# Four graph layers and a Taylor step: more tile sums on VectorE, products in pairs, row sums from a column of ones

## The reference, cut to what matters

```python
# x: (2048, 64) f32, adj: (2048, 2048) int32
# layer 1 (layer 2 the same; layer 3 holds two attentions and a small MLP): x = x + gat(relu(layernorm(x)))
Wh = inputs @ W
e = (Wh @ a_src)[:, None] + (Wh @ a_dst)[None, :]
e = jnp.where(e > 0, e, ALPHA * e)
attention = jax.nn.softmax(jnp.where(adj > 0, e, NEG_BIG), axis=1)
return jax.nn.elu(attention @ Wh)

# last layer
h = h - h.mean(axis=-1, keepdims=True)
h = h / jnp.maximum(jnp.linalg.norm(h, axis=-1, keepdims=True), EPS)
k, q = h @ w_k, h @ w_q
a = adj * softmax(k @ q.T / sqrt(8))
a = a / a.sum(axis=-1, keepdims=True)
return (a + a @ a / 2 + (a @ a) @ (a @ a) / 6) @ h
```

## Time and profile before

| | |
|---|---|
| median of the runs | 630.39 us |
| the profiled execution's own time | 626.87 us |
| its span | 625.0 us |
| TensorE busy | 550.7 us (88%) |
| VectorE busy | 401.1 us (64%) |
| ScalarE busy | 285.6 us (46%) |
| L703, products | 138.6 us |
| L695, masks | 72.9 us |
| L722, sum passes of the loops | 51.1 us |
| L929, sum passes of the last stage | 8.5 + 8.5 us |
| share of TensorE in the chain that ended last | 68% |
| share of VectorE in it | 19% |

### The profile page before, as it was taken

How to read it: one execution, slowest core, us unless ns; L and a number is a source line. 1 busy time by engine, 2 the same in 40 slices (tenths; PEclk the granted TensorE clock), 3 DMA queues, 4 the chain that set the end, 5 groups by cost and what they waited for, 6 DMA issues and landing times.

```text
span 625.0 us, 7189 instructions
## 1 busy us (share of the span) xinstructions
PE 550.7 (88%) x2951; PEld 179.8 (29%) x2986; DVE 401.1 (64%) x530; ACT 285.6 (46%) x298; POOL 32.7 (5%) x29
## 2 busy tenths in 40 slices
PE   5545999988999988999788898999769999999997
PEld 3401112233112234212133112235332232333332
DVE  2986979546988645989747988543999995100000
ACT  1475555433746433656433756344858785100000
POOL 0500000202000101000000000021100000000000
PEclk9556899999999999999999999999997999999999
DMA  8891000000000000000000000000000000000000
GB/s 356 347 404 69 1 0 2 0 1 2 0 1 0 1 1 2 2 0 1 0 1 1 1 1 1 1 1 0 2 0 1 0 1 1 1 0 1 0 1 34
DMA packets 3183, 19.30 MB, mean 31 GB/s; under 512 B 336, under 2 KB 464, under 8 KB 1104
## 3 DMA queue, kind: packets, MB, share of 16 engines
q1 hardware_dynamic: 3008, 18.04, 7.1%
q10 hardware_dynamic: 144, 0.82, 0.4%
HBM read 18.33 MB, written 0.52 MB: 30 GB/s over the span
## 4 chain that ended last, share of the span: by engine, by line
PE 68%; DVE 19%; ACT 5%; issue 4%; DMA 2%; POOL 1%; POOLq 0%; DVEq 0%; SPq 0%; ACTq 0%
PE PROD L703 15%; PE PROD L914 9%; PE X L695 9%; PE X L914 9%; PE S L722 7%; DVE X L1194 4%; DVE aB L1436 3%; ACT big L409 3%; PE S L929 2%; DVE nadj L1315 2%; DVE big L1206 2%; DMA aB<-in_adjT 1%; PE M L581 1%; PE M L678 1%; DMA cst<-in_cst 1%
## 5 line engine op out<-in xcount | busy, mean ns | idle before, releaser
L409 ACT ACTIVATE big<-X,v 128x1024 f32<-128x1024 f32 x128 | 142.6, 1114 | 132.7 <-PE X L695 132.2
L1194 DVE SCALAR_TENSOR_TENSOR X<-wB,v,aB 128x1024 f32<-128x1024 f32 x128 | 163.9, 1294 | 23.6 <-ACT big L409 21.3
L703 PE MATMUL PROD<-big,Wh 128*64 128x512 f32 x512 | 138.6, 621 | 0.4 <-ACT big L409 0.2
L695 PE MATMUL X<-nadj,bigI 128*128 128x512 bf16 x234 | 72.9, 386 | 23.5 <-DVE X L1194 21.3
L722 PE MATMUL S<-big,onesf 128*32 128x512 f32 x384 | 51.1, 604 | 3.2 <-DVE big L1206 2.4
L695 PEld LDWEIGHTS X<-nadj,bigI 128*128 128x128 bf16 x256 | 14.6, 97 | 124.1 <-DVE X L1194 87.0
L703 PEld LDWEIGHTS PROD<-big,Wh 128*64 128x64 f32 x512 | 26.1, 135 | 66.2 <-issue 58.4
L914 PE MATMUL PROD<-big,Wh 128*64 128x512 f32 x128 | 32.8, 634 | 3.3 <-ACT big L509 3.2
L342 POOL TENSOR_TENSOR rr<-var,mhalf 128x8 f32<-128x8 f32 x8 | 17.5, 2187 | 328.2 <-DVE var L1058 328.2
L914 PE MATMUL PROD<-nadj,Wh 128*64 128x512 f32 x128 | 29.8, 599 | 0.0
L1206 DVE TENSOR_TENSOR big<-big 128x1024 f32<-128x1024 f32 x24 | 29.3, 1220 | 0.4
(11 more groups left out here) (276 smaller groups left out, 586.2 us busy)
## 6 DMA issues: line engine op xcount, KB each, us to landing
big<-in_adjT SPq DMA_DIRECT2D x13, 1024.0 KB, 7.9
aB<-in_adjT SPq DMA_DIRECT2D x3, 1024.0 KB, 8.2
cst<-in_cst ACTq DMA_DIRECT2D x1, 800.0 KB, 5.4
x<-in_xT SPq DMA_DIRECT2D x1, 512.0 KB, 6.1
out<-x SPq DMA_DIRECT2D x2, 256.0 KB, 2.0
late<-in_late SPq DMA_DIRECT2D x1, 208.5 KB, 9.8
```

Of the source, the lines that this page charges most:

```text
L409: act.activation(prob[:, t % U, :], X[t % 2][:], ACT.Exp, bias=v2[l % 2][:, k:k + 1]).then_inc(p_ready, 1)
L695: last = pe.matmul(X[t % 2][:, hh * BANK:(hh + 1) * BANK], bigI[:], nadj[:, k, half_cols(c, hh)], start=False, stop=True, skip_group_check ...
L703: last = pe.matmul(PROD[c][feat(hh), :], Wh[l % 2][:, k, :], prob[:, t % U, hh * BANK:(hh + 1) * BANK], start=k == 0, stop=k == NB - 1)
L1194: dve.scalar_tensor_tensor(X[t % 2][:], wB[:, cols(c)], v8[l % 2][:, k:k + 1], aB[:, cols(c)], ALU.max, ALU.add).then_inc(x_written, 1)
```

## The change

It does three things, and a few small ones that they need.

1. **Sums.** In chunk 1 the tiles 0 to 6 are added by VectorE instead of 0 to 4: two more adds of 128x1024, behind the exponents of tiles 7 and 8. The sum pass at tile 5 goes, five passes are left there instead of six.
2. **Pairs.** In the attention loop TensorE issues product k, product k+1, mask k+2, mask k+3. Only for p = 2 the order of before stays.
3. **Row sums of the last stage.** The sum passes L929 go. The last feature of h is replaced by 1, so that the product itself carries the row sums in the last row of each half. The last feature is the negative sum of the others, since a row of h has mean zero; a matrix `restore` puts it back: `turn` multiplies with it instead of transposing for n = 0 and 1, and one more matmul of 512 columns per chunk writes the restored z to S, which VectorE adds to x (`restored`) in place of the first `scaled` addition.

```diff
-        ADDED = ((0, 1, 4, 5, 10), (0, 1, 2, 3, 4))
-        ADD_BEHIND = ({3: (1,), 6: (4,), 8: (5,), 12: (10,)}, {3: (1,), 5: (2, 3), 7: (4,)})
-        ADDS = 4
-        FIRST_SUM = (3, 5)
+        ADDED = ((0, 1, 4, 5, 10), (0, 1, 2, 3, 4, 5, 6))
+        ADD_BEHIND = ({3: (1,), 6: (4,), 8: (5,), 12: (10,)}, {3: (1,), 5: (2, 3), 7: (4, 5), 8: (6,)})
+        FIRST_SUM = (3, 7)
...
-                act.wait_ge(a_summed, c + 1)
+                act.wait_ge(q_psum, c + 1)
...
-                act.activation(sT, S[:], ACT.Copy).then_inc(rowsum_ready, 1)
+                act.activation(sT, PROD[c][:], ACT.Copy).then_inc(rowsum_ready, 1)
...
-                        for i in range(2):
-                            products(l, c, k + i)
+                        if p == 2:
+                            for i in range(2):
+                                products(l, c, k + i)
+                                mask(l, c, k + 2 + i)
+                        else:
+                            products(l, c, k)
+                            products(l, c, k + 1)
                             if p < NB // 2 - 1:
-                                mask(l, c, k + 2 + i)
+                                mask(l, c, k + 2)
+                                mask(l, c, k + 3)
...
-                for strip in range(4):
-                    tile, hh = k - 1 + strip // 2, strip % 2
-                    last = pe.matmul(S[32 * strip:32 * strip + 32, :], onesf[:, 0:32],
-                                     kept(c, tile)[:, hh * BANK:(hh + 1) * BANK], start=k == 1, stop=k == NB - 1)
...
-                    last = pe.matmul((M, X[0])[c][:, 2 * bb:2 * bb + 2], sT[:, bb * P:(bb + 1) * P], pick,
-                                     start=True, stop=True)
+                    last = pe.matmul((M, X[0])[c][:, 2 * bb:2 * bb + 2], sT[:, bb * P:(bb + 1) * P],
+                                     ident[:, F - 1::F], start=True, stop=True)
...
-                    last = pe.transpose(back[n % 2][:, bb * P:(bb + 1) * P], z[n % 2][:, bb * P:(bb + 1) * P], ident)
+                    rows = z[n % 2][:, bb * P:(bb + 1) * P]
+                    if n < NCH:
+                        last = pe.matmul(back[n % 2][:, bb * P:(bb + 1) * P], rows, restore, start=True, stop=True)
+                    else:
+                        last = pe.transpose(back[n % 2][:, bb * P:(bb + 1) * P], rows, ident)
                 last.then_inc(zT_psum, 1)
+                if n < NCH:
+                    if n:
+                        pe.wait_ge(x_restored, n)
+                    pe.matmul(S[:], restore, z[n], start=True, stop=True).then_inc(restored_psum, 1)
...
+                dve.memset(Y[1][:, b, F - 1:F], 1.0).then_inc(y0_ready, 1)
...
+            def restored(c):
+
+                dve.wait_ge(restored_psum, c + 1)
+                signal(dve.tensor_tensor(x[:, c, :], x[:, c, :], S[:], ALU.add), x_restored, c + 1)
...
+            restored(0)
             row_reciprocals(1)
             for n in range(1, 4 * NCH):
                 scaled(n)
+                if n == 1:
+                    restored(1)
```

More of the change, by code:

```diff
@@ L41 @@
 WIDTH = _at
-LATE = {"mw": (0, 3 * P), "wkq": (3 * P, 4 * EMB), "mb": (3 * P + 4 * EMB, 1)}
-LATE_WIDTH = 3 * P + 4 * EMB + 1
+LATE = {"mw": (0, 3 * P), "wkq": (3 * P, 4 * EMB), "mb": (3 * P + 4 * EMB, 1),
+        "restore": (3 * P + 4 * EMB + 1, P)}
+LATE_WIDTH = 4 * P + 4 * EMB + 1
 def program(nc, xT_d, cst_d, late_d, adjT_d, out_d):
@@ L88, in program @@
         wkq, mb, win = const("wkq"), const("mb"), const("win")
+        restore = const("restore")
         wTt = const("wTt")[0:F].rearrange("p (l k) -> p l k", l=GAT)
@@ L250, in program @@
         a_ready = sem("a_ready")
-        a_summed = sem("a_summed")
+        restored_psum = sem("restored_psum")
+        x_restored = sem("x_restored")
         rowsum_ready = sem("rowsum_ready")
@@ L276, in added_by, with additions @@
         def added_by(c_all, k):
-            return ADDS * c_all + max(ADDED[c_all % NCH].index(k), 1)
+            return additions(c_all) + max(ADDED[c_all % NCH].index(k), 1)
+        def additions(c_all):
+            return sum(len(ADDED[m % NCH]) - 1 for m in range(c_all))
         def kept(c, k):
@@ L717, in sums @@
                 if k - 1 in ADDED[c]:
-                    pe.wait_ge(p_added, ADDS * (NCH * l + c + 1))
+                    pe.wait_ge(p_added, additions(NCH * l + c + 1))
                 for strip in range(4):
@@ L815, in _ @@
                             sums(l, c, k + 1)
-                        for i in range(2):
-                            products(l, c, k + i)
+                        if p == 2:
[5 more added lines that the diff above has]
+                            products(l, c, k + 1)
                             if p < NB // 2 - 1:
-                                mask(l, c, k + 2 + i)
+                                mask(l, c, k + 2)
+                                mask(l, c, k + 3)
                             elif c == 0:
-                                mask(l, 1, i)
+                                mask(l, 1, 0)
+                                mask(l, 1, 1)
                         if c == 0 or p < NB // 2 - 1:
@@ L922, in absorb @@
                     last.then_inc(q_psum, 1)
[L923 to L926, removed]
-                for strip in range(4):
-                    tile, hh = k - 1 + strip // 2, strip % 2
-                    last = pe.matmul(S[32 * strip:32 * strip + 32, :], onesf[:, 0:32],
-                                     kept(c, tile)[:, hh * BANK:(hh + 1) * BANK], start=k == 1, stop=k == NB - 1)
-                if k == NB - 1:
-                    last.then_inc(a_summed, 1)
             def row_totals(c):
@@ L972, in _ @@
             key_rows(1)
-            pe.wait_ge(y0_ready, 1)
+            pe.wait_ge(y0_ready, 2)
             first_turn(1)
@@ L983, in _ @@
                 if k == LAG - 1:
-                    pe.wait_ge(y0_ready, 2)
+                    pe.wait_ge(y0_ready, 4)
                     max_columns(0)
@@ L1294, in first_rows @@
                 b = slice(CB * c, CB * (c + 1))
-                new = Y[1][:, b, :].rearrange("p (h b) f -> p b h f", h=2)
-                old = M[:].rearrange("p (b h f) -> p b h f", b=HB, h=2)
-                scale = ff[:, b].rearrange("p (h b) -> p b h", h=2).unsqueeze(3).broadcast_to([P, HB, 2, F])
+                new = Y[1][:, b, 0:F - 1].rearrange("p (h b) f -> p b h f", h=2)
+                old = M[:].rearrange("p (b h f) -> p b h f", b=HB, h=2)[:, :, :, 0:F - 1]
+                scale = ff[:, b].rearrange("p (h b) -> p b h", h=2).unsqueeze(3).broadcast_to([P, HB, 2, F - 1])
+                dve.memset(Y[1][:, b, F - 1:F], 1.0).then_inc(y0_ready, 1)
                 dve.tensor_tensor(new, old, scale, ALU.mult).then_inc(y0_ready, 1)
@@ L1468, in scaled @@
                     dve.wait_ge(zT_psum, n - 1)
+                    dve.wait_ge(restored_psum, min(n - 1, NCH))
                 src = PROD[c][:] if q % 2 == 0 else X[1][:, c * BANK:(c + 1) * BANK]
@@ L1471, in scaled @@
                 signal(ins, z_ready, n + 1)
-                if q != 2:
-                    coef = (1.0, 0.5, 0, 1.0 / 6.0)[q]
+                if q % 2:
+                    coef = (0.5, 1.0 / 6.0)[q // 2]
                     ins = dve.scalar_tensor_tensor(x[:, c, :], z[n % 2], coef, x[:, c, :], ALU.mult, ALU.add)
@@ L1548 @@
         put("mb", a["L2_gnn_mlp_b"].reshape(F, 1), rows)
+    restore = np.eye(P)
+    for hh in range(2):
+        restore[F * hh:F * (hh + 1), F * (hh + 1) - 1] = -1.0
+        restore[F * (hh + 1) - 1, F * (hh + 1) - 1] = 0.0
+    put("restore", restore)
     put("win", LOW + SPAN / 2 - np.arange(WIN) * (EXPS * 128))
```

## The result

The change makes the kernel slower: 644.48 us (641.1 to 647.02, 4 runs) against 630.26 (627.56 to 631.55, 4 runs), ratio 1.0228, 95% interval 1.0194 to 1.0262. That is +14.2 us where +7.0 was forecast. The time lies in the range, and in the rival whose clock falls in the loop (643 to 648.6).

A forecast was written before the change was run, and what follows sets the result against it. It took VectorE to be the later engine early in chunk 1 and TensorE the bound late in the last stage. Loops +12.6, row sums -5.7 and memsets +0.1 gave +7.0: 637.4 us against the median of 630.39, range 624 to 647.

The forecast's parts named there:

- the rival whose clock falls in the loop: Chunk 1, idle time between masks 8 and 9: TensorE drops to half rate in two to four layers, 643 to 648.6; chance 0.27.
- Adds in chunk 1: VectorE's chain from tile 5 to tile 9 gets 2.5 us longer, less about 0.5 slack; in layer 2 some 1.0 disappears.
- Pairs in chunk 1: Mask 2 comes 0.87 us later at the chain's head; behind mask 9 the pairs win about 0.4.
- Pairs in chunk 0: The 16 tiles of layer 1, laid out with pairs, lose 0.95 us; the same taken for each layer.
- Together: Adds and pairs in the loops of all four layers, chunk 0 included: 3 x 3.4 + 2.4 = +12.6 us.
- Row sums: Last stage: dropping the sum passes, less the work added for restoring the feature, nets -5.7 us.
- The stage before the second power: Last stage, first power: without the sum passes its last product ends at about 525.6, 7.15 us earlier.
- the part behind: Second power onward: longer `turn` and the added matmul to S add 0.40 + 1.05 = 1.45 us to TensorE.
- The 2.8 us priced for a fall: Loop, chunk 1: each fall of TensorE's clock means 5.7 us at half rate, a loss of 2.8.
- The sum without the clock: Whole kernel: loops, row sums and memsets give +7.0 us, so 637.4 us against the median, with no clock fall counted.

The follow-up runs named there:

- e11: The changed kernel without pairs, with filler matmuls, 7 ahead of mask 8 and 4 ahead of mask 9 of chunk 1; 631.14 us, ratio 1.0026.
- e2: The changed kernel with only the row sums kept, adds and order as before the change; 625.49 us, ratio 0.9908.
- e4: The changed kernel without the new adds, so pairs and row sums only; 631.64 us, ratio 1.0015.
- e1: The changed kernel plus eight filler matmuls of 512 columns ahead of mask 9 of chunk 1 in each layer; 635.41 us, ratio 1.0087.

## Why the prediction came out as it did

- **Adds in chunk 1** (2.5 a layer less 0.5 of slack, 1.0 less in layer 2): right. Alone they cost 1.95 in three layers and 0.92 in layer 2 (e11 against e2).
- **Pairs in chunk 1** (0.87 at the head, 0.4 back): with the adds, mask 9 came 2.42 us later after the first product in layers 0, 1 and 3, where 0.87 + 2.5 - 0.5 = 2.87 stood. Without the new adds the pairs cost 0.1 or less there and 0.6 in layer 2 (e4).
- **Pairs in chunk 0** (+0.95 a layer): in layers 1 and 3, 0.83 up to the first product of chunk 1, 0.57 at its total. In layer 2 it was 1.6. I had laid out layer 1 only and multiplied by four; layer 2 has its own order of VectorE in chunk 0 too (one mask there waits 1.42 us in e4 where it waits 0.32 in e2).
- **Together** the loops without a falling clock (e1 against e2) are longer by 8.3 in chunk 1 and by 2.8 in chunk 0 of layers 1 to 3: 11.1, where the sum without chunk 0 of layer 0 was 12.6 - 0.95 = 11.65. The mechanism that the sum is made of was right.
- **Row sums** (-5.7): 5.0 in the medians, e2 against before. The stage before the second power is 7.0 shorter in e2 (6.56 in the change), where 7.15 stood, and the part behind is 1.3 longer, where 1.45 stood; its new matmul to S took 0.95 and not 1.05.
- **The step that failed is the one I left out of the sum: "TensorE's clock falls in the loop", a rival with 0.27.** The same layout that gave +12.6 gave an idle time of 2.5 with 0.8 ahead of it in every layer. The trace had shown one fall, 2.1 us into an idle time, and gaps of 1.73 without a fall, and I put the fall at nothing in the sum although a gap of 2.5 is longer than both. It fell in four layers of four, and holding it up gave 9.1 us. The 2.8 us priced for a fall was 5.7 us at half rate; that fits layer 3 (2.82, from 5.9 us behind the restart). In the others it was 1.66, 1.66 and 1.24, since the clock came back after 3.4 us. These make 7.4 of the 9.1; the other 1.7 isn't traced, and single profiles differ by that much. The sum without the clock, 637.4, stands beside e1's 635.41, which has no fall in the loops.
- The prediction cited the Trainium skill, "TensorE: Matmul & The Clock Gate", section "HAM oscillation — how this bites in real kernels". What that section describes (a burst, a wait, then work at half rate) came in all four layers. But its waits are for DMA and longer than the 2.45 us here, so by its own condition the clock would have stayed up; the traces decide. They also differ in when: in layers 0, 1 and 2 TensorE restarted at the full clock and fell 0.7 to 1.3 us later, and only in layer 3 did it restart at half.

## What to carry to other kernels

Before moving work from a full engine to one that is "64% busy", find the stretch in which it would stand: seven added tiles with the adds of 4, 5 and 6 behind tiles 7 and 8, where VectorE was the later engine, cost 1.9 us a layer against five in three layers and 0.9 in the fourth; seven with the adds of 8, 9 and 10 behind tiles 10 and 11, where it was waiting, gained 1.9, 1.9 and 1.4, and lost 2.15 in layer 2, where it was not. So lay out every layer whose order differs. Treat every idle time that a layout gives TensorE as a possible fall of its clock, and put that into the sum. If the gap can't be removed, a few matmuls whose output nobody reads can be a cheap fix where TensorE sets the pace: 9.1 us in the loop. In the last stage, beside a VectorE that was hardly idle, they kept the clock up and brought 0.6 us in the profiles and nothing that the medians show.
